# Two transformer layers with a mixture of experts: expert tiles of 128 rows, and both attention pipelines begun with item 0

## The reference

```
x = x + L0_attn(norm(x))                        # 16 heads, a window of 32 either side
x = x + L0_xattn(ctx, norm(x), padding mask)    # keys and values: 77 context rows an item
x = x + L0_ffn(norm(x))                         # 8 experts, the best 2 of each row
x = x + L1_attn(norm(x))                        # 16 heads, causal
x = x + L1_xattn(norm(x), ctx, mask)            # the same context
x = x + L1_ffn(norm(x))                         # quantised, scales over all of x

def L0_ffn(x):
    gate_weights = softmax(x @ gate_w + gate_b)
    topk_vals, topk_idx = top_k(gate_weights, 2)
    h = gelu(x @ w1[n] + b1[n])                 # 256 -> 512, for each chosen expert n
    h = gelu(h @ w2[n] + b2[n])                 # 512 -> 512
    return sum over the 2 of topk_vals * (h @ w3[n] + b3[n])     # 512 -> 256
```

## Time and profile before

| | |
|---|---|
| median of 3 runs | 2432.71 us (2432.21 to 2432.74) |
| the profiled execution | 2430.9 us, span 2428.9 us |
| PE busy | 2154.3 us (89%), 15496 matmul records |
| DVE, ACT, POOL busy | 1260.6, 885.9, 670.3 us |
| mean granted TensorE clock | 0.952 |
| DMA | 266.86 MB, mean 110 GB/s |

### The profile page before, as it was taken

One profiled execution on the slowest core, in us unless ns is written; L12 is line 12 of the kernel. 1 busy time (PEld: TensorE's weight loads), 2 busy tenths in 40 slices (PEclk: granted clock), 3 DMA queues, 4 the chain that ended last, 5 costly groups with the idle time before them and its releaser, 6 DMA issues. The chain is left out here.

```text
span 2428.9 us, 46335 instructions
## 1 busy us (share of the span) xinstructions
PE 2154.3 (89%) x15496; PEld 1607.6 (66%) x15496; DVE 1260.6 (52%) x5376; ACT 885.9 (36%) x1511; POOL 670.3 (28%) x1192
## 2 busy tenths in 40 slices
PE   3799999999993999999999679999999999799869
PEld 2577777666662788888888456767766666344348
DVE  3677776555542210000011367788766766439974
ACT  0344444444441122222222124444544444237510
POOL 2355555134444000000000234444322211003410
PEclk9899999998985999999999779999999999899989
DMA  4332233222223555455544343333222222000013
GB/s 132 116 104 99 99 108 99 92 85 77 95 70 136 203 204 199 182 193 205 192 182 186 91 133 106 119 123 111 94 80 86 80 90 76 9 0 1 0 44 96
DMA packets 206739, 266.86 MB, mean 110 GB/s; under 512 B 57893, under 2 KB 194762, under 8 KB 201610
## 3 DMA queue, kind: packets, MB, share of 16 engines
q1 hardware_dynamic: 192986, 233.91, 27.7%
q0 software_dynamic: 9264, 27.01, 3.6%
q10 hardware_dynamic: 4352, 4.20, 0.5%
HBM read 123.21 MB, written 30.93 MB: 63 GB/s over the span
## 5 line engine op out<-in xcount | busy, mean ns | idle before, releaser
L1629 ACT ACTIVATE moe_h<-moe_h_ps,moe_weights 128x256 f32<-128x256 f32 x312 | 131.0, 471 | 442.9 <-PE moe_h_ps L1600 358.5
L1600 PE MATMUL moe_h_ps<-moe_h,moe_weights 128*128 128x256 f32 x1248 | 277.7, 381 | 0.0
L1659 DVE TENSOR_TENSOR moe_y<-moe_y_ps,moe_weights 128x512 f32<-128x512 f32 x39 | 27.0, 692 | 482.4 <-PE moe_y_ps L1611 482.4
L1081 ACT ACTIVATE causal_prob<-causal_ps 128x768 f32<-128x768 f32 (+1 forms) x192 | 169.1, 881 | 248.5 <-PE causal_ps L1264 247.5
L1600 PEld LDWEIGHTS moe_h_ps<-moe_h,moe_weights 128*128 128x128 f32 x1248 | 235.6, 191 | 30.8
L2031 PE MATMUL ffn_prod_ps<-x_sb,ffn_weights 128*128 128x512 f32 x480 | 210.6, 598 | 9.7 <-ACT ffn_sig_q L2017 7.0
L832 DVE CUSTOM_DVE_ANT_0 causal_masked<-causal_ps,causal_causal_mask 128x256 bf16<-128x256 f32 (+1 forms) x512 | 152.1, 353 | 67.6 <-PE causal_ps L1228 67.2
L1561 POOL DMA_DIRECT2D moe_y_dram<-moe_y x39 | 29.6, 760 | 560.1 <-DVE moe_y L1659 560.1
L2031 PEld LDWEIGHTS ffn_prod_ps<-x_sb,ffn_weights 128*128 128x128 f32 x480 | 90.9, 191 | 127.1 <-issue 110.0
L832 DVE CUSTOM_DVE_ANT_0 window_masked<-window_ps,window_window_mask 128x160 bf16<-128x160 f32 x512 | 135.3, 320 | 63.1 <-PE window_ps L1228 61.3
L1584 PE MATMUL moe_h_ps<-moe_rowsT,moe_weights 128*128 128x256 f32 x624 | 143.6, 384 | 1.2 <-DVE moe_rowsT L1648 1.2
(11 more groups left out here) (347 smaller groups left out, 4504.9 us busy)
## 6 DMA issues: line engine op xcount, KB each, us to landing
moe_weights<-moe_w_in SPq DMA_DIRECT2D x39, 2180.0 KB, 8.5
q_pair<-window_q_parts SPq DMA_DIRECT2D x256, 128.0 KB
q_pair<-causal_q_parts SPq DMA_DIRECT2D x256, 128.0 KB
k_pair<-window_k_parts SPq DMA_DIRECT2D x128, 128.0 KB
k_pair<-causal_k_parts SPq DMA_DIRECT2D x128, 128.0 KB
moe_rows<-moe_slots_dram SPq DMA_DIRECT2D x39, 256.0 KB, 2.8
moe_y_dram<-moe_y POOLq DMA_DIRECT2D x39, 256.0 KB, 2.5
k_pair<-window_k_parts SPq DMA_DIRECT2D x128, 38.5 KB
```

Of the source, the lines that this page charges most:

```text
L1081: nc.scalar.activation(out, src, ACT.Exp).then_inc(expd, 1)
L1600: op = nc.tensor.matmul(h2_ps[:, f // 2, (f % 2) * TM:(f % 2) * TM + TM], w2[:, k, f * P:f * P + P], h1[:, k, :], start=(k == 0), stop=(k ...
L1629: nc.scalar.activation(out[:, f, :], psum[:, f // 2, (f % 2) * TM:(f % 2) * TM + TM], ACT.Gelu, bias=bias[:, f:f + 1]).then_inc(done, 1)
L1659: nc.vector.tensor_tensor(y[r][:], y_ps[:, r, :].rearrange("p (s d) -> p s d", s=TS), b3.unsqueeze(1).to_broadcast([P, TS, D]), ALU.add).t ...
```

## The change

Three things are changed. In the experts `TM` is 128, so `MT` is 71; there are four weight buffers and two banks for y (`YR`); the raw weights are quantised a third at a time, beside tiles 2, 3 and 64 to 69. In `attention` everything that item 0 doesn't need moves behind what it needs: one `loaded` and one `scaled` semaphore a kind, SP loads kind 0's weights first, then (in the first pipeline) the rest of the first quarter of x, the context, kind 1's weights, the rest of x and the gate's weights; DVE takes the statistics and scales kind 0 alone; the context is turned at the end of step 0 in pairs of tiles, and copied by ACT; each kind's bias product is done inside step 0 or 1; POOL sets most constants behind item 0's deviation; ACT loads its table by a `warm` activation. In the second pipeline POOL gathers item 0 first, and items 1 and 2 behind item 0's normalisation. In `layers` only two tiles of x are loaded ahead, and the clearing of `q_pair` and `k_pair` is left out.

```diff
-TM = 256
+TM = 128
...
-        loaded = sem("loaded")
+        loaded = [sem(f"loaded{i}") for i in range(NL)]
...
+                load_layer(0)
+                if load:
+                    x_view, _, x_second, x_loaded = load
+                    sp.dma_start(x_sb[:, ST:TILES // 4, :], x_view[:, ST:TILES // 4, :]).then_inc(x_second, 16)
+                if merge:
+                    sp.wait_ge(got_in[0], 64)
                 for L in crosses:
                     whole = CTX_TILES - 1
                     sp.dma_start(L.ctx_rows[:, 0:whole, :],
...
+                for r in range(1, NL):
+                    load_layer(r)
+                if load:
+                    for n in range(1, 4):
+                        quarter = slice(n * TILES // 4, (n + 1) * TILES // 4)
+                        sp.dma_start(x_sb[:, quarter, :], x_view[:, quarter, :]).then_inc(x_loaded, 16)
...
                 if merge:
                     gather(0, 0)
+                else:
+                    layernorm(0, 0)
+                constants()
+                if route:
+                    route_constants()
+                if merge:
+                    layernorm(0, 0)
                     gather(1, 1)
-                layernorm(0, 0)
-                if merge:
                     gather(2, 2)
...
+                        late = bool(merge) and ref == 0
+                        if i == 4 and late:
+                            for n in range(4):
+                                merge_rows(1, 1, n)
+                        if i == (4 if late else 1) and active(ref, -1):
                             stats(t + 1, ref + 1)
...
+                        if i == 5 and ref < NL:
+                            widen(ref)
+                    if ref == 0:
+                        dve.wait_ge(consts, 1)
+                        for r in range(1, NL):
+                            scale_layer(r)
...
+                def widen(r):
+
+                    L = layers_in[r]
+                    if L.biased:
+                        n = with_bias.index(L)
+                        if n:
+                            dve.wait_ge(bias_mm, n)
+                        nc.vector.tensor_copy(bv_wide[:], L.bv[:].unsqueeze(2).to_broadcast([P, KC, P])).then_inc(widened, 1)
+                        dve.wait_ge(bias_mm, n + 1)
+                        nc.vector.tensor_copy(L.out_bias[:], pso[:, r, 0:D]).then_inc(bias_done, 1)
...
-RING = 3
+RING = 4
+YR = 2
...
-                        if not first_turn(j):
-                            pe.wait_ge(y_done, j - (RING - 1))
+                        wait(pe, y_done, j - (YR - 1))
...
+                    def beside(j):
+                        if j == 0:
+                            compact()
+                        for m in range(3):
+                            if j == (2, 2, 3)[m]:
+                                find_scales(m)
+                            if j == (3, MT - 7, MT - 7)[m]:
+                                divide(m)
+                            if j == (MT - 6, MT - 6, MT - 5)[m]:
+                                round_off(m)
+                            if j == (MT - 5, MT - 4, MT - 4)[m]:
+                                clip(m)
+                            if j == (MT - 3, MT - 3, MT - 2)[m]:
+                                rescale(m)
...
-                for n in range(4):
-                    tiles = slice(n * TILES // 4, (n + 1) * TILES // 4)
-                    sp.dma_start(x_sb[:, tiles, :], x_view[:, tiles, :]).then_inc(x_loaded, 16)
-                sp.wait_ge(x_loaded, 64)
...
+                sp.dma_start(x_sb[:, 0:ST, :], x_view[:, 0:ST, :]).then_inc(x_first, 16)
```

More of the change, by code:

```diff
@@ L176, in __init__, with attention @@
         self.rows_dram, self.peak = rows_dram, peak
-def attention(nc, layers_in, x_sb, q_pair, k_pair, v_aug, ident, selects, eye, merge=None, tail=None, route=None):
+def attention(nc, layers_in, x_sb, q_pair, k_pair, v_aug, ident, selects, eye, merge=None, tail=None, route=None, load=None):
     NL = len(layers_in)
@@ new lines, in _ @@
+                if load:
[3 more added lines that the diff above has]
+                if route:
+                    with nc.allow_non_contiguous_dma(reason="eight columns"):
+                        sp.dma_start(gate_w[:], route.weight.rearrange("(k p) e -> p k e", p=P)).then_inc(route_loaded, 16)
+                        sp.dma_start(gate_b[:], route.bias.rearrange("(o e) -> o e", o=1).to_broadcast([P, NE]))\
+                          .then_inc(route_loaded, 16)
@@ L495, in store, with halve_masks @@
+                def halve_masks():
+                    for r, L in enumerate(layers_in):
+                        if L.mask_key is None:
+                            continue
+                        sp.wait_ge(scaled[r], 1)
+                        nat = L.mask_nat[-1][:]
+                        for part in rows_of:
+                            for half in range(2):
+                                sp.dma_start(L.mask_key[part, half, :], nat[rows_of[half], :]).then_inc(halved, 16)
                 def store(t, ref):
@@ L1081, in exponentials, with copy_context @@
                         nc.scalar.activation(out, src, ACT.Exp).then_inc(expd, 1)
-                act.wait_ge(scaled, 1)
-                act.wait_ge(consts, 1)
+                def copy_context():
+                    n = 0
+                    for L in crosses:
+                        for first in range(0, CTX_TILES, 2):
+                            cols = min(2 * P, B * S2 - first * P)
+                            n += 1
+                            act.wait_ge(ctx_turned, n)
+                            nc.scalar.activation(L.ctxT[:, :, first * P:first * P + cols],
+                                                 ctx_ps(n - 1)[:, :, 0:cols], ACT.Copy).then_inc(ctx_copied, 1)
                 def see(t, ref):
@@ L1553, in load_raw @@
                                          a[f"L1_ffn_w_{name}"].rearrange("(f p) n -> p f n", p=P)).then_inc(raw_in, 16)
[L1555 removed]
+                    tiles(sp, tile, load_raw)
                 @block.gpsimd
@@ L1698, in _, with divide @@
-                    tiles(dve, tile, {0: compact, 1: find_scales, 2: divide, MT - 3: round_off, MT - 2: rescale})
+                        link(nc.vector.tensor_reduce(wmax[:, part], blocks(m), AX.X, ALU.max, apply_absolute_value=True))
+                        link(nc.vector.tensor_scalar(wscale[:, part], wmax[:, part], 1.0 / 7.0, LEAST, ALU.mult, ALU.max))
+                        link(nc.vector.reciprocal(winv[:, part], wscale[:, part]))
+                    def divide(m):
+                        link(nc.vector.tensor_tensor(blocks(m), blocks(m), each(winv, m), ALU.mult))
@@ L1703 @@
+                    tiles(dve, tile, beside)
 FI = 768
@@ L2144, in _ @@
             def _(dve):
-                for i in range(2):
-                    nc.vector.memset(k_pair[i][:].bitcast(F32), 0.0)
                 dve.wait_ge(filled, 1)
```

357 lines of the change are left out of this document (183 added, 174 removed).

## The result

The changed kernel takes 2365.06 us, the median of four runs (2361.15 to 2370.18), against 2432.72 before (2432.21 to 2435.07): a ratio of 0.9721, 95% interval 0.9701 to 0.9742. That is 67.7 us less; 64.6 were forecast, and 2368.0. The profiled execution takes 2366.39, its span 2364.8, 64.1 less than before; the other 3.6 us are mostly the places of the two profiled executions among the runs (1.8 under the median before, 1.3 above it after).

A forecast was written before the change was run, and what follows sets the result against it. The prediction took TensorE to bound the experts and waiting chains to bound both attention beginnings. Gains of 29.7, 26.6 and 8.3 sum to 64.6 us, taking 2432.7 to 2368.0 us, with a range of 2348 to 2400.

The forecast's parts named there:

- Experts, 29.7: Experts stretch: shorter tiles, 71 at 7.32 us, take it from 555.3 to 525.6 us, gaining 29.7 us.
- a pass of 0.112: Experts, TensorE: a pass moving 128 columns takes 0.112 us, floored by loading the 128x128 stationary operand.
- DVE's stalls: Experts: quantisation queued on DVE beside four tiles delays TensorE by 4.5 us in all, taken as 5.
- First attention, 26.6: Start of the first attention: first scores at 34.5 us, 29.6 earlier, less 3 for the second bias product: 26.6 gained.
- TensorE's context turning: First attention, step 0: context transposes after the bias product end at 34.5 us and set the first scores.
- SP's queue: First attention: loads queued ahead let the first stacks through by 33 us, or 37 as a bound.
- Second attention, 8.3: Start of the second attention: first maximum 10.8 us earlier, less 2.5 for the bias product: 8.3 gained, bounds 3 and 12.
- The bias product's step: Second attention, step 1: the bias product moved into it costs 2.5 us.
- loads that don't overlap: Rival, SP's queue in the experts: each tile costs one whole landing, 8.5 us, total 2447 us; chance 0.04.
- a middle period: Rival, experts: tiles of 7.6 to 8.0 us from dearer passes, DMA jitter or DVE's queue, total 2402 us; chance 0.17.
- the clock fell: Rival, experts: TensorE drops to 1.2 GHz for a tenth of the time, 50 us more, total 2418 us; chance 0.03.
- the beginnings: Starts of both attentions, 34.9 us gained together; the rival had them give half, total 2385 us, chance 0.10.

The follow-up runs named there:

- e4: The changed kernel with the experts' first and second layers moving only 64 of a tile's 128 rows from tile 4 on: 2354.86 us in one run.
- e7: The changed kernel with SP issuing x's last three quarters and the gate's weights behind item 1's stacks instead of ahead of item 0's: 2360.89 us.
- e8: The changed kernel with the second bias product moved from step 1 to the end of step 0 in both attention pipelines: 2364.37 us.
- e3: The changed kernel with three weight buffers instead of four, keeping two banks for y: 2536.07 us.
- e11: The changed kernel with three weight buffers instead of four and three banks for y instead of two: 2532.88 us.
- e5: The changed kernel with 12 of the second layer's 16 products left out of every expert tile, loads unchanged: 2282.2 us in one run.
- e1: The kernel before with only the experts of the change (128-row tiles, four weight buffers, quantisation by thirds): 2404.95 us.
- e12: The changed kernel unaltered, measured again on the same chip as the runs beside it: 2366.76 us.
- e9: The changed kernel with quantisation spread over more tiles, x's rest and gate weights loaded later, and the first attention's second bias product in step 0: 2354.2 us.
- e10: e9 plus identity matmuls that nothing reads on TensorE ahead of item 0 in both attention pipelines (16 and 30): 2355.82 us.

## Why the prediction was right

The forecast's four numbers, each beside what the profiled execution shows:

- **Experts, 29.7.** 555.3 became 525.6, the forecast to a tenth, and each piece of it holds: a pass of 0.112, a tile of 7.31 for 7.32, DVE's stalls 5.7 us for the 4.5 that I had worked out and rounded up to 5. That it comes to the tenth is luck: 0.7 less for the period and 0.7 more for the stalls. The price of a pass came from eight loads of another product and not from its columns; e4, and the stream of 8 columns, show that the columns do not set it. The DMA share was to be near 0.85 and is 0.89.
- **First attention, 26.6.** The first scores came 28.0 us earlier, 29.6 forecast, and step 1 lost 2.5 us to its bias product, 3 forecast. From item 4 to item 22 each item turns 25.2 to 25.3 us earlier. The sum is 1.4 off, but its working named the wrong one of two candidates: I took TensorE's context turning (to 34.5) to be the later one and SP's queue (33, or 37 as a bound) the earlier. TensorE was done at 29.5: the bias product began at 25.4 for 26.7 and took 1.7 us for 3.4, and the context took 2.4 for the 4.4 that I had priced at half clock, where its passes start 0.12 us apart. SP's queue set 36.12, as the bound had it, and e7 proves it: with SP free the scores come at 28.7.
- **Second attention, 8.3.** The first scores lie 37.9 us behind the experts' end in place of 50.4: 12.4 earlier, and the first maximum 11.1 (40.1 for 51.2), 10.8 forecast. The bias product's step costs 4.6 more than before's (24.72 for 20.10), 2.5 forecast. At item 2's turn 7.3 are left, and at the last item's 8.4 for the forecast of 8.3; other executions of the same code there lie up to 2 us from it (664.4 us from the experts' end to the last item's turn in after, 662.3 in e7). Without the product step 1 takes 20.60 (e8), so 4.1 of the 4.6 hang on it. Of these, the two groups of scores around it lie 5.4 us apart for 2.1 in e8, 3.3 more: it takes 2.6 us at a mean clock of 0.60, where it takes 1.7 in the first attention. How the rest comes about I did not settle.
- **The rest.** 23.6 us were gained up to the first second layer, 29.9 from it to the experts' end (1356.4 and 1302.95), and 10.6 behind it: 64.1. Of the 10.6, 2.2 lie behind the last item's turn, where the work is the same: 397.4 us for 399.6, with a granted clock of 0.96 for 0.95. Over all traces here that stretch takes 397.4 to 400.7, so the 2.2 are luck, and they make up for what the first attention's later steps lost (25.3 gained at item 22, 23.6 at the first second layer). That the sum comes within 0.5 of the forecast in this execution owes something to both.

The rivals: loads that don't overlap need their buffers taken away to appear (e3, e11); a middle period had less ground than I gave it (e5); the clock fell for no tile of after's experts behind the first, though e1, e4 and e8 each show one such fall; the beginnings gave 25.2 and 8.4, 33.6 of 34.9.

**The spread that I had not counted.** The four runs of the changed kernel differ by 9 us; those of before beside them by 3, but later ones also by 9 (2430.13 to 2438.81). All kernels here have the same place where executions differ most. Windows of two neighbouring steps of the cross attention in after, where a steady step has the same instructions:

```profile
587.30:607.10 19.80, 17.85 (x172) 13.23 (x170) 11.14 (x43) 9.95 (x18) 9.34 (x21) 1.00 0.30 97
607.10:630.00 22.90, 21.10 (x173) 15.26 (x171) 11.36 (x43) 9.94 (x18) 9.36 (x21) 0.85 0.26 81
```

At full clock a step is 19.85 us, with a spell at half 21.4 to 23.9. The eight steps from item 23 to item 31 take 169.3 us in before, 173.3 in after, 169.9 in e12, 163.9 in e4 and 174.0 in e9; at full clock they would take 158.8. Which steps are hit changes from one execution to the next, in before as in after. So a difference of 4 us between two profiles is read from the stage in which the edit stands, never from the totals. For instance, e9's profiled run (2363.27), the slowest of its four, still has the short begin and the short experts that its edits give; the other three have no trace to compare. What starts a spell was not found.

## What to carry to other kernels

Where the stationary operand stays 128 by 128 in float32, fewer moved columns stop paying at 128: here a pass costs 0.11 us with 128 columns, with 77, with 64 and with 8, so a smaller tile pays only by the padding that it saves, against more loads. Before making tiles shorter, count what the old length covered: each engine's odd work has to fit in the shorter cover (2.6 us of DVE here), and one more buffer decides whether the loads stay hidden. At a kernel's begin read each queue in order: what item 0 needs was ready, and stood 5.4 us behind transfers that item 4 is the first to need.

## What the runs showed of the hardware

- Two and more queued loads reached 424 GB/s at a DMA share of 1.01 (e5); the stretch before that I had taken for the full rate gave 384 at 0.91.
- The granted clock reads 1.00 at the begin of the program although TensorE is slow. In e9 and e10 the same projection, windows 15.70:19.50 and 15.30:17.30, takes 3.78 and 1.99 us:

```profile
15.70:19.50 3.80, 3.72 (x9) 3.00 (x10) 1.00 (x4) 0.03 (x1) 0.89 (x2) 1.00 1.08 346
15.30:17.30 2.00, 1.92 (x9) 1.71 (x10) 0.90 (x4) 0.03 (x1) 0.00 (x0) 1.00 1.07 369
```

  The column can't tell these two apart; the starts of the passes do. In the second pipeline of e10 it reads 0.50 for the projection of 3.78 us.
- One DMA issue of SP for a small load took 2.91 us (gate_w at 23.99), where it takes 0.38 in before, behind a wait for the large loads. In after three loads of 1 MB stand directly ahead of it; in e7 they do so at another place, and it takes 2.76 there (at 53.60). Behind such loads a small one was not cheap in any trace here.
